# Causal attention on half the rows per pair of heads: 64-row products in pairs, maxima as rows of the queries, one product for both parts of the values, units of 1,024 columns

## What is computed

```python
q = q * cos + _rotate_half(q) * sin
k = k * cos + _rotate_half(k) * sin
scores = jnp.einsum('bhqd,bhkd->bhqk', q, k) * scale
causal = jnp.triu(jnp.ones((seq_len, seq_len), dtype=bool), k=1)
scores = jnp.where(causal, -jnp.inf, scores)
probs = jax.nn.softmax(scores, axis=-1)
out = jnp.einsum('bhqk,bhkd->bhqd', probs, v)
...
for e in range(E):
    out = out + combine[:, e:e + 1] * (x_flat @ expert_w[e].T)
```

## Time and profile before

| | us |
|---|---|
| device time, median of 3 runs | 739.61 |
| lowest, highest | 734.37, 740.0 |
| span of the profiled execution (first to last instruction) | 735.1 |
| its own device time | not given apart from the span |
| TensorE busy | 627.9 (85%) |
| VectorE busy | 467.8 (64%) |
| ScalarE, GpSimd busy | 346.7, 249.1 |
| mean granted clock of TensorE | 0.930 |

### The profile page before, as it was taken

The page is one execution under the profiler, slowest core; times in us unless marked ns, Lnnn a source line. Parts: engine busy times, 40 slices in busy tenths (PEclk is TensorE's granted clock), DMA queues, the critical chain, the costliest instruction groups (busy, mean ns, idle before and its releaser), DMA issues.

```text
span 735.1 us, 20283 instructions
## 1 busy us (share of the span) xinstructions
PE 627.9 (85%) x8800; PEld 528.4 (72%) x8800; DVE 467.8 (64%) x1032; ACT 346.7 (47%) x549; POOL 249.1 (34%) x260
## 2 busy tenths in 40 slices
PE   5739999999999999565797778898989898988867
PEld 4638787888878787354686656687878787877755
DVE  2577768686777778314554534686868686867445
ACT  4444455463737473116876235544454535361610
POOL 1010203212130303003876518363635454543430
PEclk9878999999999999785998978899999999999997
DMA  7203001010120000001124031221304040400000
GB/s 280 80 1 128 17 3 54 3 56 23 35 69 3 2 3 2 1 1 43 35 68 73 15 58 45 30 61 28 71 18 73 16 74 16 74 16 1 16 15 16
DMA packets 16889, 29.78 MB, mean 41 GB/s; under 512 B 1952, under 2 KB 10400, under 8 KB 15904
## 3 DMA queue, kind: packets, MB, share of 16 engines
q1 hardware_dynamic: 16800, 28.49, 15.5%
HBM read 22.19 MB, written 6.29 MB: 39 GB/s over the span
## 4 chain that ended last, share of the span: by engine, by line
PE 37%; DVE 9%; ACT 3%; POOL 3%; issue 2%; DVEq 0%; POOLq 0%; ACTq 0%
PE ps L203 22%; DVE mx L1419 3%; PE ps L1150 3%; PE ps L1102 3%; PE ps L1013 2%; PE ps L1128 2%; PE ps L1131 2%; PE ps L1105 1%; PE ps L1134 1%; DVE acc L1509 1%; DVE st L1358 1%; ACT prob L1267 1%; DVE t L1464 1%; ACT tn_mlp L1194 1%; DVE cl_moe L1369 1%
## 5 line engine op out<-in xcount | busy, mean ns | idle before, releaser
L1342 POOL TENSOR_TENSOR e2l<-prob,e2h 128x1536 f16<-128x1536 f32 x32 | 98.7, 3102 | 16.7 <-ACT e2h L1273 16.7
L203 PE MATMUL ps<-secondh,ch_moe 128*128 128x256 f16 (+1 forms) x320 | 82.5, 265 | 3.4 <-DVE cl_moe L1369 3.1
L516 PE MATMUL ps<-yh,wconvh 128*128 128x256 f16 x288 | 80.3, 279 | 4.2 <-POOL yl L675 4.2
L203 PE MATMUL ps<-secondh,cl_moe 128*128 128x256 f16 (+1 forms) x320 | 82.8, 265 | 0.0
L203 PE MATMUL ps<-secondl,ch_moe 128*128 128x256 f16 (+1 forms) x320 | 82.7, 265 | 0.0
L516 PE MATMUL ps<-yh,wconvl 128*128 128x256 f16 x288 | 80.3, 279 | 0.0
L675 POOL TENSOR_TENSOR yl<-y,yh 128x128 f16<-128x128 f32 x32 | 13.1, 444 | 197.9 <-ACT yh L622 197.9
L516 PE MATMUL ps<-yl,wconvh 128*128 128x256 f16 x288 | 80.0, 278 | 0.0
L1419 DVE TENSOR_REDUCE mx<-ps 128x2 f32<-128x512 f32 (+1 forms) x96 | 65.6, 683 | 22.5 <-PE ps L1105 22.5
L1267 ACT ACTIVATE prob<-ps 128x1536 f32<-128x1536 f32 x32 | 46.5, 1452 | 44.7 <-PE ps L1134 44.7
L1509 DVE SCALAR_TENSOR_TENSOR acc<-ps,gate,acc 128x256 f32<-128x256 f32 x112 | 49.1, 480 | 27.0 <-PE ps L203 27.0
(11 more groups left out here) (222 smaller groups left out, 2090.3 us busy)
## 6 DMA issues: line engine op xcount, KB each, us to landing
weights_stage<-in_second SPq DMA_DIRECT2D x6, 684.0 KB, 4.1
qs<-rope_scratch SPq DMA_DIRECT2D x24, 128.0 KB, 3.7
ks<-rope_scratch SPq DMA_DIRECT2D x24, 128.0 KB, 5.4
weights_stage<-in_wconv SPq DMA_DIRECT2D x6, 384.0 KB, 4.5
xw<-in_xw SPq DMA_DIRECT2D x8, 256.0 KB, 2.8
xc<-in_xc SPq DMA_DIRECT2D x8, 256.0 KB, 3.1
rope_scratch<-rh SPq DMA_DIRECT2D x8, 256.0 KB, 2.3
rope_scratch<-rl SPq DMA_DIRECT2D x8, 256.0 KB, 2.3
```

The source lines that it names most:

```text
L203: last = nc.tensor.matmul(out_ap, lhs[x], rhs[w], start=done == 0, stop=done == n - 1)
L516: last = nc.tensor.matmul(bank(p, 2 + oh)[:, 0:TOK], w["wconv"][:, c0:c0 + P], im[:, h, dy:dy + HW, dx:dx + HW], start=(tap, h, n) == (0, ...
L1342: nc.gpsimd.tensor_tensor(el[n % 2][:], prob[n % 2][:], eh[n % 2][:], ALU.subtract).then_inc(e2_lo, 1)
```

## The change

- **Rows.** `qs` and `ks` hold half the heads on partitions 0 to 49 and half on 64 to 113. Each product contracts at most 64 rows, and two products for two heads stand next to each other, one on the upper and one on the lower half of the rows, into two banks (`pair_products`). The mask becomes two products of 64 rows and 64 columns a head, for each half.
- **Units.** Six units of two banks (1,024 columns) an image replace twelve steps of maxima and four groups of 1,536 columns of weights. Maxima use banks 0 and 1 of `psum[0]`, weights 2 and 3.
- **Maxima.** They are written to a new `max_scratch` in DRAM and read back as rows 48, 49 (and 112, 113) of the queries; the keys hold constant factors there. The products with `headb` fall away. SyncE gets a step `shift_rows` with one write and two reads an image, and `stack` issues twelve transfers of 64 KB in place of six of 128 KB.
- **Values.** High and low parts lie side by side (33 columns): 24 products a group, of 33 and 17 columns. VectorE adds the two parts in a copy (`mid`) before it divides.
- **Order.** Both lists are new. The fill of slots -3 to -1 is later and shorter, `rotate` and `stack` move a slot earlier (lag -3), the first unit of maxima too (lag -2), `out_project` to its own slot's end.
- In `windows` only the copies of the mask constants change.

```diff
-    ("load", 0), ("widen", 4), ("mlp_normalise", 2), ("mlp_base", 2), ("mlp_low", 3), ("narrow", 5),
-    ("statistics", 5), ("tokens", 1), ("mlp_channels", 2)]
-FILL_FROM, FILL_SLOT, FILL_END = 4.25, 3.0, 31.0
+    ("mlp_normalise", 3), ("mlp_base", 5), ("tokens", 2), ("load", 1), ("mlp_channels", 3), ("statistics", 6),
+    ("widen", 4), ("mlp_low", 3), ("narrow", 5)]
+FILL_FROM, FILL_SLOT, FILL_END = 6.75, 2.0, 62.5
 IMAGE_SLOT = [
-    ("out_project", 1), ("store", 2), ("moe_statistics", 1), ("split", 0, 0), ("maxima", -1, 0), ("attend", 0,
-    1), ("maxima", -1, 1), ("maxima", -1, 2), ("rotate", -2, 0), ("moe_normalise", 1), ("split", 0, 1),
-    ("maxima", -1, 3), ("norm_channels", 1), ("attend", 0, 2), ("logits", 1), ("rotate", -2, 1), ("expert", 1,
-    0), ("attend", 0, 3), ("stack", -2), ("maxima", -1, 4), ("weigh", 0, 0), ("expert", 1, 1), ("rotated_low",
-    -2), ("maxima", -1, 5), ("split", 0, 2), ("expert", 1, 2), ("weigh", 0, 1), ("maxima", -1, 6), ("expert", 1,
-    3), ("maxima", -1, 7), ("split", 0, 3), ("expert", 1, 4), ("maxima", -1, 8), ("values", -2), ("maxima", -1,
-    9), ("weigh", 0, 2), ("expert", 1, 5), ("maxima", -1, 10), ("expert", 1, 6), ("maxima", -1, 11),
-    ("qkv_normalise", -3), ("weigh", 0, 3), ("out_channels", 0), ("shifts", -1), ("shift_rows", -1), ("expert",
-    1, 7), ("out_split", 0), ("qkv_channels", -3), ("attend", -1, 0), ("qkv_low", -3)]
+    ("qkv_normalise", -3), ("moe_statistics", 1), ("maxima", -1, 1), ("values", -2), ("moe_normalise", 1),
+    ("attend", 0, 0), ("maxima", -1, 2), ("norm_channels", 1), ("split", 0, 0), ("attend", 0, 1), ("split", 0,
+    1), ("logits", 1), ("store", 1), ("expert", 1, 0), ("qkv_channels", -3), ("qkv_low", -3), ("attend", 0, 2),
+    ("maxima", -1, 3), ("split", 0, 2), ("expert", 1, 1), ("attend", 0, 3), ("expert", 1, 2), ("weigh", 0, 0),
+    ("split", 0, 3), ("maxima", -1, 4), ("attend", 0, 4), ("rotate", -3, 0), ("expert", 1, 3), ("weigh", 0, 1),
+    ("split", 0, 4), ("attend", 0, 5), ("maxima", -1, 5), ("expert", 1, 4), ("expert", 1, 5), ("weigh", 0, 2),
+    ("split", 0, 5), ("rotate", -3, 1), ("expert", 1, 6), ("weigh", 0, 3), ("expert", 1, 7), ("out_channels",
+    0), ("shifts", -1), ("shift_rows", -1), ("stack", -3), ("out_split", 0), ("rotated_low", -3), ("maxima", -2,
+    0), ("out_project", 0)]
...
-        SCORE_BANKS = [((0, 1, 2, 3), P, 0), ((0, 1), TOK, P), ((2, 3), TOK, P)]
-
-        WEIGHT_BANKS = [((0, 1), 0, 0), ((2, 3), 0, 0), ((0, 1, 2, 3), P, P)]
-
-        rows_zeroed = sem("rows_zeroed")
+        UNITS = [(P, 0, 4), (TOK, 0, 2), (TOK, 2, 2), (P, 4, 4), (TOK, 4, 2), (TOK, 6, 2)]
+        NU = len(UNITS)
+        LONG = [n for n, (width, _, _) in enumerate(UNITS) if width == TOK]
+        E_BUFFER = [n // 3 if n % 3 == 0 else 1 + n % 3 for n in range(NU)]
+
+        def pair_of(at):
+            return psum[0][:, at * BANK:(at + 2) * BANK]
+
+        def e_free(eng, c, n):
+
+            if n in LONG:
+                freed(eng, pv2, c * GROUPS + LONG.index(n) - 1)
+            else:
+                freed(eng, pv2, (c - 1) * GROUPS + n // 3 * 2 + 2)
...
-                freed(sp, weights2, (c - 1) * GROUPS)
+                freed(sp, weights2, (c - 1) * NU)
                 sp.wait_ge(spilled[p], (c // 2 + 1) * 32)
                 for qk, dst, parts in ((0, qs, (0, 1, 0)), (1, ks, (0, 0, 1))):
                     for n, part in enumerate(parts):
                         src = scratch[p, part, qk * 2:qk * 2 + 2].rearrange("j (d h) t -> (j d) (h t)", h=L1H)
-                        sp.dma_start(dst[p][n * L1D:(n + 1) * L1D].rearrange("r h t -> r (h t)"), src)\
-                            .then_inc(stacked[p], 16)
+                        for side in range(2):
+                            r0 = side * HALF + n * L1D
+                            sp.dma_start(dst[p][r0:r0 + L1D].rearrange("r h t -> r (h t)"),
+                                         src[:, side * SLOTS * TOK:(side + 1) * SLOTS * TOK]).then_inc(stacked[p], 16)
+
+            def shift_rows(c):
+
+                p = c % 2
+                sp.wait_ge(shift_done, c + 1)
+                sp.dma_start(max_scratch[p], shift[p][:]).then_inc(max_spilled[p], 16)
+                freed(sp, weights2, (c - 1) * NU)
+                sp.wait_ge(max_spilled[p], (c // 2 + 1) * 16)
+                for side in range(2):
+                    r0 = side * HALF + KSTACK
+                    sp.dma_start(qs[p][r0:r0 + 2].rearrange("r h t -> r (h t)"),
+                                 max_scratch[p, side * L1H:(side + 1) * L1H].rearrange("(s h) t -> s (h t)", s=2))\
+                        .then_inc(max_stacked[p], 16)
...
+            def pair_products(at, n, left, l0, right, r0, rows, part, diagonal):
+
+                width, s0, count = UNITS[n]
+                for m in range(count):
+                    for side in range(2):
+                        own = slice(side * HALF, side * HALF + rows)
+                        nc.tensor.matmul(bank(0, at + side)[:, m * width:(m + 1) * width], left[own, s0 + m, l0:l0 + P],
+                                         right[own, s0 + m, r0:r0 + width], start=m == 0, stop=False)
+                at_part = part * 2 * P
+                triangle = masks[:, 4 * P + part * HALF:4 * P + (part + 1) * HALF]
+                for half in range(2):
+                    for side in range(2):
+                        own = slice(side * HALF, (side + 1) * HALF)
+                        to = bank(0, at + side).rearrange("p (h m) -> p h m", m=width)
+                        c0 = diagonal + half * HALF
+                        last = nc.tensor.matmul(to[:, :, c0:c0 + HALF],
+                                                masks[own, at_part + half * P:at_part + (half + 1) * P],
+                                                triangle[own].unsqueeze(1).to_broadcast([HALF, count, HALF]),
+                                                start=False, stop=half == 1)
+                return last
...
+                        pe.wait_ge(t1_done, B)
+                        pe.wait_ge(affine2, B * 2)
+                    pe.wait_ge(stacked[p], (c // 2 + 1) * 12 * 16)
                     freed(pe, shift_done, c)
                 else:
-                    pe.wait_ge(max2, c * GROUPS * 3 + n)
-                to = bank(1, 1)
-                for m, h in enumerate(heads):
-                    nc.tensor.matmul(to[:, m * keys:(m + 1) * keys], qs[p][:, gr * GH + h, q0:q0 + P],
-                                     ks[p][:, gr * GH + h, 0:keys], start=m == 0, stop=False)
-                diagonal = to.rearrange("p (h m) -> p h m", m=keys)[:, :, keys - P:keys]
-                nc.tensor.matmul(diagonal, identb[:], maskb[:].unsqueeze(1).to_broadcast([P, len(heads), P]),
-                                 start=False, stop=True).then_inc(scores2, 1)
+                    pe.wait_ge(max2, c * NU + n)
+                long = n in LONG
+                pair_products(0, n, qs[p], P if long else 0, ks[p], 0, KSTACK, 1, P if long else 0).then_inc(scores2, 1)
...
-                pe.wait_ge(e2_lo, n + 1)
-                freed(pe, o2_done, n)
+                pe.wait_ge(e2_lo, c * NU + LONG[gr] + 1)
+                freed(pe, recip2, n)
+                long, short = E_BUFFER[LONG[gr]], E_BUFFER[gr // 2 * 3]
                 for t in range(TILES):
                     for h in range(GH):
-                        c0 = (t * GH + h) * D1
-
-                        blocks = [h * TOK] if t == 0 else [h * TOK + P, 2 * BANK + h * P]
-                        for kt, e0 in enumerate(blocks):
-                            for m, (e, v, w) in enumerate(((eh, vh, D1), (eh, vl, L1D), (el, vh, D1))):
-                                last = nc.tensor.matmul(bank(0, 3)[:, c0:c0 + w], e[n % 2][:, e0:e0 + P],
-                                                        v[c % 3][:, kt, gr * GH + h, 0:w], start=(kt, m) == (0, 0),
-                                                        stop=(kt, m) == (len(blocks) - 1, 2))
+                        c0 = (t * GH + h) * D2
+                        side, m = divmod(h, 2)
+
+                        blocks = [(long, side * BANK + m * TOK + t * P)]
+                        if t == 1:
+                            blocks.append((short, side * BANK + (gr % 2 * 2 + m) * P))
+                        for kt, (e, e0) in enumerate(blocks):
+                            v = v2[c % 3][:, kt, gr * GH + h]
+                            nc.tensor.matmul(bank(1, 1)[:, c0:c0 + D2], eh[e][:, e0:e0 + P], v, start=kt == 0, stop=False)
+                            last = nc.tensor.matmul(bank(1, 1)[:, c0:c0 + D1], el[e][:, e0:e0 + P], v[:, 0:D1],
+                                                    start=False, stop=kt == len(blocks) - 1)
...
+            def attend(c, n):
+
+                u = c * NU + n
+                freed(act, e2_lo, u - 1)
+                act.wait_ge(weights2, u + 1)
```

(31 more changed lines are left out.)

## The result

The changed kernel takes 729.87 us (median; 728.26 to 733.99) where the one before took 739.81 beside it: a ratio of 0.989, 95% interval 0.986 to 0.993 (the two medians alone divide to 0.987). It is faster by 1.1%, where I had forecast 702 us, 5.1%, and a range that ended at 721. Its profiled execution took 733.99, with a span of 732.1.

What follows compares the result with a forecast made beforehand. TensorE was taken to bound the steady slots. Gains of 23, 5, 4, 6 and 2 us, less 2 for the clock, took 38 off the 735.1 span: 697, device time 702; own range 692 to 712, 8 in 10 between 683 and 721.

Steps and rivals of the forecast that it cites:

- VectorE 28.1 us a slot: VectorE's busy time in slots 1 to 5 rises from 26.45 to 28.1 us, above TensorE's 26.8.
- slots 1 to 5: The steady image slots fall from 35.56 to 31.0 us each, a gain of 23 us.
- the signs that it named for being wrong: Head over 15 us, maxima over 1.4 us, or granted clock in the slots under 0.95.
- The head, 13.1 us from the last expert to expert 0: Start of a slot: expert 0's products start 13.1 to 13.4 us after the last expert's start on TensorE.
- The clock, 2 us: Lower granted clock in the slots' heads: a loss of 2 us in all, against 7.5 at clock 0.61.
- Slot 0, 25 us: Slot 0, cast to cast and without experts, falls from 30.9 to 25 us, a gain of 6.
- Slots 6 and 7, 9 us: Last two slots: 33.43 to 28.3 us and 30.26 to 26.2, gains of 5 and 4.
- The MLP and the fill, 2 us: Stage before slot 0, same products in another order: 2 us saved for shorter maxima, bounds −8 and +8.
- The trip of the maxima through DRAM: Write and read-back of the maxima: TensorE waits 1.6 us before unit 0's weights; the head does not move.
- From span to device time: Median device time taken as 4.5 us above the profiled span: span 697, device time 702.
- The clock rival: Chance 0.15: clock 0.61 in the head, 0.93 in the rest, costing 2.8 us a slot: 720 us.
- "little gain": Chance 0.05: chain and engines meet no better; the fill costs 8 us, slots come to 34: 730 us.

Runs made afterwards that it cites:

- serial: Changed kernel with each unit's products for one half of the rows all before those for the other, instead of in turn: 728.6 us.
- three_warm: late9_three plus 24 products a slot that nothing reads (6, 10, 8), where TensorE waits in the head: 709.8 us.
- mid_psum: Changed kernel with the sum of the weighted values' two parts written to PSUM, so that the division reads one input there: 715.5 us.
- both2: mid_psum with the gate's equality and its product by the constant also kept in the logits' PSUM bank, which both comparisons read: 714.1 us.
- late9_three: late9_mid with three buffers for the exponentials in place of two: 712.8 us.
- late9_mid: mid_psum with GpSimd's first subtraction of a slot waiting for the whole gate of the image before (nine steps): 715.3 us.
- late: Changed kernel with GpSimd's first subtraction of a slot waiting for four steps of the gate of the image before: 722.6 us.
- warm_both: both2 plus 24 products a slot that nothing reads (6, 10, 8), where TensorE waits in the head: 710.4 us.

## Why the prediction was wrong

**What held.** *A pair costs one product:* eight products of 128 columns start within 0.23 us (541.78 to 542.01), a long unit's masks within 0.21 (540.15 to 540.36), forecast 0.44 for the short unit; taking turns between the halves isn't what does it (serial). *TensorE 26.8 us a slot:* in three_warm, at full clock, 29.73 with 24 unread products of 0.11, so 27.1. *Maxima 1.21 us:* 1.214 in the mean. *VectorE 28.1 us a slot:* 27.3 in three_warm, where little is held. *The read-back of q and k:* nothing waited for it in the changed kernel. *The weight loads:* by the rule of the Trainium skill, TensorE: Matmul & The Clock Gate, Part 3, that the prediction names, they would have cost 7 us; no load shows in the units' 0.23.

**What failed, in the order of the sum.** Gains in us, the forecast's, then measured in the profiles of the changed kernel and of three_warm:

| term | forecast | changed kernel | three_warm |
|---|---|---|---|
| slots 1 to 5 | 23 | −1.8 | 15.2 |
| slot 6 | 5 | 0.8 | 0.5 |
| slot 7 | 4 | −1.6 | −1.0 |
| the last experts | 0 | 3.0 | 4.2 |
| slot 0 | 6 | −0.7 | −1.0 |
| MLP and fill, ahead of the cast | 2 | 10.4 | 11.9 |

The forecast took 2 off again for the clock. Its 23 also starts too high: it counts slot 1 as 35.56, where that slot took 32.0 before (466.15 to 498.14); slots of 31 would have gained 19.6. Of the signs that it named for being wrong two came, a head over 15 us and a clock under 0.95.

*The price of the division and of the gate.* I took 0.29 us from the earlier trace rows for each added operation of 128 columns, and left the division and the gate at their price. But the division of the earlier trace rows reads PSUM (`o<-ps,rs`), the new one reads SBUF twice, and the new order sets the gate beside GpSimd's subtractions, where it stood at their end before. VectorE is 31.7 us a slot in place of 28.1: the weighing's part is shown, 11 to 14 us (mid_psum); freeing part of the gate as well is worth 3 more (both2), all of it with a third buffer 3.9 (late9_three).

*The head, 13.1 us from the last expert to expert 0.* In the changed kernel these products start at 530.84 and 547.20, 16.4 apart; in late9_mid, with nothing held, at 520.94 and 534.74, 13.8. So the walk was right but for the holds: there the division ends late and TensorE waits 1.67 us for it. And I let the walk end at the products. The update behind them waits for the gate, 6.3 us in the changed kernel and 2.9 in late9_mid, and the later experts wait for the update. I listed what GpSimd does only as a sum (18 to 19 us) and as a deadline; I never set its start against VectorE's row.

*The clock, 2 us.* The direction was right, the size too small. In the heads of slots 1 to 6 (last update to expert 0's update) it is 0.77 to 0.91, in slot 7 0.65, neither the 1.00 of the sum's products nor, but for slot 7, near the rival's 0.61. In slot 2's head TensorE is busy 13.78 us of 18.15 at 0.81, where before it was 14.18 of 16.16 at 1.00. The unread products give about 1.5 us back in each full slot where nothing else holds it, the rival's price for its chain, but only 2 to 3 over the whole stretch.

*Slot 0, 25 us.* It took 31.6, and 30.5 to 32.7 in the variants. My walk left out what the chain shows there: 24 products of `narrow` for the last image, 4.62 us at half clock, a step of 1.28 us on ScalarE ahead of its first exponential, and a division held for 1.95. With the clock raised behind `narrow` it didn't move, so there the order of ScalarE's, GpSimd's and VectorE's work sets it; which step isn't taken apart.

*Slots 6 and 7, 9 us.* They gained nothing, in three_warm neither. In the changed kernel the head of slot 7 alone takes 19.2 us to expert 0's update, with both comparisons held and the clock at 0.65. The rest of the reason stays open.

*The MLP and the fill, 2 us.* Its products were priced alike in another order; it gave 10, beyond the bound of 8. This is the whole gain of the median, and no step of the working foresaw it.

*The trip of the maxima through DRAM.* I expected TensorE to wait 1 to 2 us for it in each slot. In slots 1 to 5 it never did: in one of them the write is issued at 536.23, the read-back at 537.66, and unit 0's weights start at 541.78 with no wait. In slots 6 and 7 it waited 0.6 and 0.5 us.

*From span to device time.* The 4.5 us added at the end are not a property of the kernel: in every run here the device time is 1.7 to 2.0 us over the span, and the rest was a profiled execution faster than the median.

**The account.** Of the 36 us missing in the image stretch, 18.2 came back in three_warm (281.9): 11.2 by the division, the rest by the gate, the third buffer and the clock, which overlap. Of the other 18, by the table, 8 are slots 1 to 5 (3.6 of them the wrong start of the sum), 9.5 slots 6 and 7 and 7 slot 0; the last experts give 4 back, and the 2 us for the clock were counted already. In three_warm slots 2 to 4 take 32.8 us for 31.0, and GpSimd's delayed subtractions are 11.5% of a slot's chain, 3.8 us. So their gap may be the price of that cure; I haven't found an order in which GpSimd is both early and out of the gate's way, and this stays open.

**The rivals.** The clock rival gave 720 and had the right sign; "little gain" gave 730 and met the number by luck, for the opposite reason (slots of 34 and a fill that costs 8 us; here slots 2 to 4 were 35.5 to 37 and the fill gave 10). The engines' sums were right, and the mechanism of the miss was in none of them: an interaction of two engines that each sum leaves out.

## What to carry to other kernels

When an order is changed or an operand moves from PSUM to SBUF, list for each VectorE operation where its inputs lie and what GpSimd does at that time: two inputs in SBUF beside a GpSimd operation cost its rest, up to 2.2 us here for a 0.28 us operation, while one input in PSUM cost nothing. Moving one operation out of the hold only hands it to the next one; free the whole chain, or the time in which it runs. When two engines' sums come close (28 and 27 us here), a slot is their chain and not the larger sum; of 8 us added to either some 4 showed in the image stretch. And measure a long program by stages: here the slots that the change was made for gained nothing, and a stage beside them gave the whole gain.

## What the runs showed of the hardware

- The hold is that of a whole instruction: in every row shown VectorE's operation ends 0.04 to 0.15 us after GpSimd's, however short it is; also one of 16 columns, 0.17 us alone, took up to 1.94 (late).
- One operation with a single input took as long as if held too: the maxima's scaling from f32 to f16, beside GpSimd's addition (428.57, 2.34 us), and it ended 0.04 us after it. The mean of this line over eight was 450 ns, the others ran at 0.18.

```profile
428.62 2.33 DVE L1457 TENSOR_SCALAR mx2h<-mx 128x32 f16<-128x32 f32 x1
```

- 24 unread products a slot, put where TensorE waits, raised the granted clock of a full slot from 0.90 to 1.00 and shortened it from 34.4 to 32.5 us (both2, warm_both).
- 64-row products on different halves of the rows overlap whether they come in turn or half after half: a unit of 2,048 columns was through within 0.66 us, for 0.85 one behind the other (changed kernel, serial).
